# Cross-attention and a routed feed-forward on one core: last unit of an odd step behind the up products, combine weights turned one step later, other orders in the first stage and the tail

## The reference, cut to what matters

```python
x = x + xattn(layernorm(x), ctx_1024, Wq, bq, Wk, bk, Wv, bv)   # 16 batches of 112 rows, 375 keys, width 256
x = x + ffn(layernorm(x), w_router, w_gating, w_gate, w_up, w_down)

def ffn(x):                                    # 8 experts, hidden width 1024, all experts for all rows
    router_probs = softmax(x @ w_router)
    gate_weights = softmax(x @ w_gating / 0.1)
    g, u = x @ w_gate[e], x @ w_up[e]          # for each expert e
    expert_out = (silu(g) * u) @ w_down[e]
    cw = router_probs * gate_weights
    cw = cw / (sum(cw) + 1e-9)
    return sum over e of expert_out[e] * cw[e]
```

## Time and profile before

| | us |
|---|---|
| median of 3 runs | 1003.21 (1002.66 to 1003.54) |
| the profiled execution | 1002.24 |
| its span, first to last instruction | 1000.5 |
| TensorE busy | 979.5 (98%), 5188 matmuls |
| GpSimd, VectorE, ScalarE busy | 791.5, 750.7, 485.5 |

### The profile page before, as it was taken

One profiled execution on the slowest core, in us unless ns is written; L12 is line 12 of the kernel. 1 busy time (PEld: TensorE's weight loads), 2 busy tenths in 40 slices (PEclk: granted clock), 3 DMA queues, 4 the chain that ended last, 5 costly groups with the idle time before them and its releaser, 6 DMA issues. The chain is left out here.

```text
span 1000.5 us, 14885 instructions
## 1 busy us (share of the span) xinstructions
PE 979.5 (98%) x5188; PEld 896.4 (90%) x5188; DVE 750.7 (75%) x1280; ACT 485.5 (49%) x857; POOL 791.5 (79%) x618
## 2 busy tenths in 40 slices
PE   8999999999999999999999999999999999999998
PEld 7999898988988998899998899998898888999887
DVE  7987456777777777788777777777887777777775
ACT  6887554444544444544445344445444454444441
POOL 4789975766878798888888787988888887879752
PEclk9999999999999999999999999999999999999999
DMA  8341232311001110011100110111101100111202
GB/s 211 98 126 45 61 95 82 95 60 41 22 22 42 41 50 33 22 61 40 43 22 22 42 59 22 35 48 40 43 22 55 46 22 22 42 40 47 67 1 74
DMA packets 43426, 51.59 MB, mean 52 GB/s; under 512 B 2980, under 2 KB 39304, under 8 KB 43352
## 3 DMA queue, kind: packets, MB, share of 16 engines
q1 hardware_dynamic: 43344, 50.64, 16.6%
q10 hardware_dynamic: 8, 0.00, 0.0%
HBM read 45.07 MB, written 5.56 MB: 51 GB/s over the span
## 5 line engine op out<-in xcount | busy, mean ns | idle before, releaser
L318 PE MATMUL ps<-arena 128*128 128x448 f32 (+5 forms) x2112 | 398.3, 339 | 3.6 <-DVE w_raw L1388 1.8
L561 POOL TENSOR_TENSOR arena<-shared,arena 128x448 fp32r<-128x448 f32 x196 | 257.7, 1329 | 152.1 <-ACT arena L920 145.8
L318 PEld LDWEIGHTS ps<-arena 128*128 128x128 f32 (+2 forms) x2112 | 351.0, 187 | 27.7 <-DVE w_raw L1388 2.0
L318 PE MATMUL ps<-xc_hi,w_hi 128*128 128x448 f32 x904 | 335.4, 371 | 10.6 <-DVE shared L1291 8.4
L318 PE MATMUL ps<-xc_hi,w_lo 128*128 128x448 f32 x904 | 331.3, 367 | 0.0
L318 PE MATMUL ps<-xc_lo,w_hi 128*128 128x448 f32 x904 | 331.2, 366 | 0.0
L913 ACT ACTIVATE shared<-shared 128x448 f32<-128x448 f32 x180 | 102.8, 580 | 204.5 <-DVE shared L1301 127.3
L318 PEld LDWEIGHTS ps<-xc_hi,w_hi 128*128 128x128 f32 x904 | 169.9, 188 | 35.2 <-DVE shared L1291 18.6
L318 PEld LDWEIGHTS ps<-xc_hi,w_lo 128*128 128x128 f32 x904 | 170.1, 188 | 14.7
L318 PEld LDWEIGHTS ps<-xc_lo,w_hi 128*128 128x128 f32 x904 | 170.0, 188 | 13.8
L673 POOL TENSOR_TENSOR xsacc<-xsacc,xf 128x448 f32<-128x448 f32 x104 | 119.1, 1155 | 2.4 <-DVE xf L1381 2.4
(11 more groups left out here) (164 smaller groups left out, 1165.2 us busy)
## 6 DMA issues: line engine op xcount, KB each, us to landing
early<-in_L_ffn_w_down SPq DMA_DIRECT2D x16, 512.0 KB, 4.0
xf<-cw_dram SPq DMA_DIRECT2D x16, 448.0 KB, 4.7
shared<-in_ctx SPq DMA_DIRECT2D x16, 336.0 KB
w_raw<-in_L_ffn_w_gate SPq DMA_DIRECT2D x17, 256.0 KB, 2.8
w_raw<-in_L_ffn_w_up SPq DMA_DIRECT2D x17, 256.0 KB, 3.2
early<-in_L_ffn_w_gate SPq DMA_DIRECT2D x15, 256.0 KB, 2.8
early<-in_L_ffn_w_up SPq DMA_DIRECT2D x15, 256.0 KB, 3.1
x_dram<-xsacc SPq DMA_DIRECT2D x8, 224.0 KB, 2.5
```

The costliest lines, as they stand in the source:

```text
L318: ins = nc.tensor.matmul(dst, w, m, start=first and i == 0, stop=last and i == len(passes) - 1, skip_group_check=onto)
L561: nc.gpsimd.tensor_tensor(h[:, 1, j, at:at + TC], tile, h[:, 0, j, at:at + TC].bitcast(fp32), ALU.subtract).then_inc(hid_lo_done, 1)
```

## The change

- TensorE, odd steps of the turned groups: `unit(g, 3)` stands behind up 4 and up 3, the end of the step, where it stood behind up 2 and up 7, ahead of gate 4 and gate 3.
- VectorE, even steps: `weigh(g - 1, 3)`, the product with that unit, stands ahead of `gate_u2`, where it stood behind it.
- `turn_cw` stands in step 5 behind its first three gate products, where it stood ahead of step 4; `keep_cw` follows in step 5 behind `gate_u2`. The wait for `keep_cw` moves from the first matmul of step 4 to up product 5 of step 5.
- The tail: `add_back(1, 1)` stands on VectorE between `hidden11` and `hidden22` of the last step, where it stood behind the whole step.
- The router weights: `split_router` on VectorE becomes `router_high` on ScalarE and `router_low` on GpSimd.
- The lists of the first stage stand in another order on all five engines. There are ten `keep_busy` before and after, at other places. SyncE loads Wq and Wk ahead of the first rows of x.

```diff
@@ SyncE, first stage
-            load_x(0)
             load_weights(0)
             load_weights(1)
+            load_x(0)
+            load_ctx_half(0, 0)
             load_x(1)
-            load_ctx_half(0, 0)
+            load_bv()
...
@@ GpSimd and ScalarE, new functions
+            def router_low():
+                pool.wait_ge(wr_hi_done, 1)
+                nc.gpsimd.tensor_tensor(wr_split[:, :, 1, :], wr_raw[:], wr_split[:, :, 0, :].bitcast(fp32),
+                                        ALU.subtract).then_inc(wr_done, 1)
+            def router_high():
+                sc.wait_ge(router_in, 2 * DMA)
+                nc.scalar.copy(wr_split[:, :, 0, :], wr_raw[:]).then_inc(wr_hi_done, 1)
@@ VectorE
-            def split_router():
-                ve.wait_ge(router_in, 2 * DMA)
-                nc.vector.tensor_copy(wr_split[:, :, 0, :], wr_raw[:]).then_inc(wr_hi_done, 1)
-                ve.wait_ge(wr_hi_done, 1)
-                low(wr_split[:, :, 1, :], wr_raw[:], wr_split[:, :, 0, :]).then_inc(wr_done, 1)
...
             sums_1_3(1)
-            keep_cw()
-
             def quad(n):
                 g, odd = n // FPAIRS - 1, n % FPAIRS
+                if not odd and g - 1 in TURNED:
+                    weigh(g - 1, 3)
                 gate_u2(n)
+                if n == PLAIN + 1:
+                    keep_cw()
...
-                elif g - 1 in TURNED:
-                    weigh(g - 1, 3)
-                else:
+                elif g - 1 not in TURNED:
                     add_rows(g - 1, 4, ps_r[4])
...
                 hidden11(n)
+                if n == QUADS - 1:
+                    add_back(1, 1)
                 hidden22(n)
...
-            add_back(1, 1)
             add_rows(GROUPS - 2, 4, ps_r[4])
@@ TensorE
                 if n == PLAIN:
-                    pe.wait_ge(cw_kept, 1)
...
                 product(n, 1, 6, u_x, True).then_inc(up_prod, 1)
+                if n == PLAIN + 1:
+                    pe.wait_ge(cw_kept, 1)
                 product(n, 1, 5, u_y, True).then_inc(up_prod, 1)
...
             def turn_cw():
                 pe.wait_ge(cw_ready, 1)
-                pe.wait_ge(logits_done, CP)
+                pe.wait_ge(up_sum, 5)
...
                 gate_1_6_5(n)
+                if n == PLAIN + 1:
+                    turn_cw()
...
                 up_2_7(n)
-                if odd and turned:
-                    unit(g, 3)
...
                 up_4_3(n)
+                if odd and turned:
+                    unit(g, 3)
...
-            turn_cw()
             for n in range(PLAIN, QUADS):
                 quad(n)
```

More of the change, by code:

```diff
@@ L615, in _ @@
             root2(3)
+            cn_low(6, 1)
             norm2(3)
-            cn_low(6, 1)
+            low_part(0, "first")
             cn_low(7, 0)
-            low_part(0, "first")
+            add_bv(7)
             low_part(0, "second")
             cn_low(7, 1)
+            root2(4)
             low_part(0, "s13")
-            root2(4)
+            norm2(4)
+            sum_s4()
             low_part(0, "s2")
-            sum_s4()
-            norm2(4)
+            root2(5)
+            norm2(5)
             sum_of_set(3, 0)
@@ L630, in _ @@
             sum_of_set(3, 3)
-            root2(5)
-            norm2(5)
+            root2(6)
             plain_low(0, 0)
-            root2(6)
+            norm2(6)
             plain_low(0, 1)
-            add_bv(7)
-            norm2(6)
-            low_part(1, "first")
             root2(7)
@@ L641, in _ @@
             norm2(7)
+            low_second6()
+            low_part(1, "first")
             plain_low(0, 3)
             plain_low(1, 0)
-            plain_low(1, 1)
-            low_second6()
-            plain_low(1, 2)
             sum_of_set(2, 0)
@@ L650, in _ @@
             sum_of_set(2, 3)
+            plain_low(1, 1)
+            plain_low(1, 2)
+            low_down(0)
             plain_low(1, 3)
-            low_down(0)
             plain_low(2, 0)
@@ L959, in _ @@
             cn_high(2, 0)
+            router_high()
             ct_high(3, 0)
+            high_set(1)
             exponentials(2, 0)
-            cn_high(2, 1)
[L963 to L969, removed]
+            exponentials(2, 1)
+            normalise(1)
+            q_high(3)
+            pt_high(2, 0)
+            ct_high(3, 1)
+            cn_high(2, 1)
+            cn_high(3, 0)
             pt_high(2, 1)
             norm1(4)
-            cn_high(3, 0)
             ct_high(4, 0)
@@ L976, in _ @@
             exponentials(3, 0)
+            at_high(1)
+            exponentials(3, 1)
+            cn_high(4, 0)
+            pt_high(3, 0)
+            q_high(4)
+            ct_high(4, 1)
+            pt_high(3, 1)
             normalise(2)
[L978 to L981, removed]
             norm1(5)
-            pt_high(3, 1)
-            cn_high(4, 0)
+            ct_high(5, 0)
+            exponentials(4, 0)
+            xt_high(5)
+            at_high(2)
             cn_high(4, 1)
[L986 to L989, removed]
             exponentials(4, 1)
+            ct_high(5, 1)
+            keep_norm2(0)
             pt_high(4, 0)
-            keep_norm2(0)
-            ct_high(5, 1)
             normalise(3)
@@ L1433, in _ @@
             m_low()
+            xt_low(0)
             both_biases()
@@ L1988, in _ @@
             queries(0)
+            keep_busy(1)
+            keep_busy(1)
             transpose_ctx(1, 0)
+            transpose_norm(1)
+            keep_busy(1)
             scores(0, 0)
-            transpose_norm(1)
             scores(0, 1)
```

349 lines of the change are left out of this document (172 added, 177 removed).

## The result

| | before | after |
|---|---|---|
| median, in turn on one chip | 1003.38 us (4 runs) | 986.86 us (983.87 to 989.22, 4 runs) |
| the profiled execution | 1002.24 | 986.00 |
| its span | 1000.5 | 984.2 |

The ratio is 0.9832 (95% interval 0.9803 to 0.9862): 16.5 us faster, where 15.2 were forecast.

What follows compares the result with a forecast made beforehand. TensorE, busy in 98% of the span, was taken as the bound, with gate_u2 waits the loop's culprit. Terms -6.8 - 3.5 - 1.1 - 1.7 - 2.0 = -15.1 us gave 988 from the median 1003.21; forecast 985 to 991, chance 0.50.

Steps and rivals of the forecast that it cites:

- Which wait bounds the loop: Loop: TensorE waits 27 times for VectorE's gate_u2; these waits hold 15.3 us, which moving unit 3 removes.
- What is late next: Odd steps: up 4 and up 3 wait for VectorE's sums, 0.31 or 0.26 us in 28 steps; 8.5 us come back.
- The first rival: Odd steps: up 4 is in time, so no 8.5 us come back and the kernel takes 979.6; chance 0.10.
- The cover of `gate_u2`: Even steps: gate_u2's sum is done before TensorE reaches gate 7, with about 0.6 us to spare.
- the fourth rival: Odd steps: hidden22 is held up to 2.05 instead of 0.62, the gate_u2 wait returns: 1013 us; chance 0.06.
- The loop's sum: Loop: 15.3 us of removed waits less 8.5 us of new ones, net -6.8 us.
- a rival (983, 996): Second rival, loop: matmul spacing becomes 0.203 us throughout (983) or 0.207 throughout (996) instead of mixed; chance 0.17.
- The start: Steps 4 and 5: the wait for the combine weights' copy and the clock's fall go, -3.5 us net.
- the fifth rival: Start of the loop: the clock falls all the same, elsewhere; 1.6 us are lost, 990; chance 0.07.
- The new wait of up 5: Step 5: up product 5 waits for the copy of the combine weights and comes 0.3 us late, bounds 0 and 2.2.
- The tail: After the loop: turn_back(0, 1) no longer waits, -1.1 us; down(30, 6) no longer waits for add_back(1, 1), -1.7 us.
- The first stage: First 40 us: new order and the router split off VectorE give -2.0 us, range -4.5 to +4.5.

Runs made afterwards that it cites:

- the loop part alone: Unit 3 behind up 3 of the odd step and its weigh ahead of gate_u2, on the kernel before: 990.25 us, ratio 0.9886.
- The run with two more operations: Two more VectorE reductions of 448 columns ahead of gate_u2 in each even step of a turned group, on the 973.28 us kernel: 990.94 us.
- the step to 973 us: weigh(g, 2) put behind up_u3_c22 in the odd steps, on the kernel after: 973.28 us, ratio to before 0.9710.

## Why the prediction was right, point by point

- **Which wait bounds the loop.** Right. The 27 waits by `gate_u2` are gone in the kernel after, and the loop part alone does that.
- **What is late next.** Right in place and size: 28 short waits at up 4 and up 3, released by `up_u3_c22`, 0.32 and 0.26 us where 0.31 and 0.26 stood. The run with `weigh(g, 2)` behind the sum shows that this one operation makes it late. The first rival, up 4 in time (979.6), falls.
- **The cover of `gate_u2`.** In time, as forecast, but about 0.6 was forecast and 0.9 is in the trace at the narrow spacing. From the end of up 3's sum to gate 7 it is 7.46 us (forecast 7.5). From the same point VectorE's sum ends after 6.49, where the forecast had 6.8 (434.3; the 433.7 beside it is the sum's start). The forecast took the distances between starts over from the rows; in the kernel after, the operation behind `hidden12` starts 1.51 us after it and not 1.70, and the second of the chain 0.53 after the first and not 0.62. `hidden22` kept its short form in all turned odd steps (0.62 to 0.77), so the fourth rival, 1013, did not come. The run with two more operations shows its mechanism: a delay beyond the cover is paid in full, with 0.10 on top. Its price was too high: with 0.9 to spare instead of 0.6, a delay of 1.43 would have cost about 0.6 in each pair, by an estimate from these numbers, and not 0.9.
- **The loop's sum** came out as -7.6 instead of -6.8. The step that was mis-sized is the mixture of spacings: 10 of 28 stretches were wide before, 8 of 27 after. I took the mixture as constant and gave both ends a rival (983, 996). That it came out nearly constant is partly luck: the same loop of before had 10, 6 and 3 wide stretches in three profiles, 2.5 us apart. That it is the waits which keep a mixture alive was in my reach, since I wrote that the spacing changes only at a wait; I did not draw from it that a kernel without waits could be narrow from end to end. It made the loop part alone 3.9 us better than forecast and the step to 973 us 5 us better.
- **The start.** -3.6 for -3.5 in the profiles, 3.1 (3.6 by its profile) when undone. The clock stays at its upper level, 2.4 GHz, through step 4, and all four runs of the kernel after have a mean granted clock of 1.000, so the fifth rival falls. The turn's part doesn't do this alone: with only the turn moved, the clock did fall elsewhere, in the profiled run behind the tail's gap, which the kernel after no longer has. The new wait of up 5 came: the matmul ahead of it is followed 0.41 later instead of 0.20, and its successor 0.31, where 0.3 was forecast. The later load of the next weight set showed in no wait.
- **The tail.** -1.3 and -1.9 for -1.1 and -1.7; the second is confirmed by the run that undoes it (1.8).
- **The first stage.** -1.9 for -2.0 in the two profiles, 0.6 to 3.3 by the runs of it alone. My argument was that VectorE is relieved of the split. That holds, and the split was dearer than its said: VectorE spends 2.2 us on its two operations in the profile of before and 4.6 in two others of the same code, and putting them back costs 1.4. That the size agrees is luck: it was a choice inside wide bounds, and executions of the old first stage differ by up to 5 us.

## What to carry to other kernels

Count a wait of the busiest engine twice: what it lasts, and what it does to the work behind it. Here 28 waits of 0.3 us cost about 13 us together. When a wait is moved away, look at the operation that stands directly ahead of the sum that is late next: one `weigh` of 0.53, put behind the sum, was worth 13.6 us, beside 16.5 for the whole change. And a small operation with two SBUF inputs doesn't belong on VectorE while GpSimd works: 1.8 to 3.6 us there, 0.25 on GpSimd. Last, read the granted clock of every run and not only of the profiled one: here it told apart executions of one kernel that lie 2 us from each other.

## What the runs showed of the hardware that I had not expected

- Matmuls of 448 columns, each with its own weights, follow each other every 202.7 ns or every 206.7 ns, with the same granted clock of 1.00. In the first form the distances repeat with a period of five (207, 203, 202, 203, 199 ns), in the second they are even (207, 207, 206). A stretch keeps its form until TensorE waits: over 127 to 130 matmuls between two waits in all kernels, and over 3,668 without one. I found no rule for which form follows a wait. With the loop part alone the first five distances behind the wait were the same to 1 or 2 ns at 24 waits in a row, and the stretch behind each was narrow. And a wide stretch was followed by a narrow one in all cases but one. Narrow instead of wide is worth 0.5 us in each pair of steps.
- An idle gap of 2.2 us, with no gap ahead of it, was followed by 3 to 4 us at 1.2 GHz at the start of the loop in all four profiled kernels that had it (granted clock 0.72 to 0.76 in windows of 6 to 7 us). Gaps of nearly the same length in the tail (1.8) were followed by it once in five profiles: with the turn moved alone, the granted clock was 0.57 from 984 to 988 us. Nor does it come in every execution: of 39 runs of the kernel before whose clock is on record, 7 have a mean of 1.000, that is no such fall, and their median is 1000.4 us, that of the other 32 is 1002.9.

```profile
984.00:988.00 4.00, 4.00 (x23) 4.00 (x22) 1.36 (x3) 0.00 (x0) 0.68 (x1) 0.57 0.20 66
```
- The router split's subtraction on VectorE, 128 x 32 with two SBUF inputs, ended 0.05 us behind a GpSimd instruction in all five profiles that have it. In three it outlasted one of them (1.78, 1.78 and 1.87 us); in two GpSimd's next one followed at once, and the subtraction outlasted that too (3.56 and 3.55 us).
